# An audio layer whose first norm's factor is carried by the second norm's epsilon: what it does to the time

## The reference, cut to what matters

```
x = x * rsqrt(mean(x^2) + 1e-6) * w_pre        # per token, over 2560
h = x @ w1.T                                   # 1024 numbers
g = silu(h[512:]) * h[:512]                    # gate times value
y = g @ w2.T                                   # 1024 numbers
y = y * rsqrt(mean(y^2) + 1e-6) * w_post       # per token
```

## Time and profile before

| | us |
|---|---|
| median of 3 runs | 2608.62 |
| the 3 runs | 2606.7 to 2609.98 |
| the profiled execution's own time | 2612.99 |
| its span, first to last instruction | 2611.3 |
| PE busy in the span | 2454.8 (94%) |
| DVE busy in the span | 1663.6 (64%) |
| mean granted clock of PE | 0.97 of full speed |

### The profile page before, as it was taken

One profiled execution on the slowest core, in us unless ns is written; L12 is line 12 of the kernel. 1 busy time (PEld: TensorE's weight loads), 2 busy tenths in 40 slices (PEclk: granted clock), 3 DMA queues, 4 the chain that ended last, 5 costly groups with the idle time before them and its releaser, 6 DMA issues. The chain is left out here.

```text
span 2611.3 us, 45875 instructions
## 1 busy us (share of the span) xinstructions
PE 2454.8 (94%) x15004; PEld 2124.4 (81%) x15004; DVE 1663.6 (64%) x3316; ACT 1191.6 (46%) x3624; POOL 984.6 (38%) x852
## 2 busy tenths in 40 slices
PE   8999999986899978999999999799999998899998
PEld 6888788875566658899999999678888886899998
DVE  8875587893466658889999898621111112877775
ACT  5664445441344448898989898611111111111110
POOL 5764677771122226666666666200000000111110
PEclk9999999997899989999999999899999999899999
DMA  7654677676456541111111110453333332211211
GB/s 253 199 166 146 190 247 250 210 230 235 129 177 210 187 140 65 45 44 44 41 46 42 45 46 36 143 166 97 96 96 96 96 96 81 89 65 65 81 65 49
DMA packets 202314, 313.61 MB, mean 120 GB/s; under 512 B 20784, under 2 KB 157488, under 8 KB 202032
## 3 DMA queue, kind: packets, MB, share of 16 engines
q1 hardware_dynamic: 194256, 282.54, 33.8%
q0 software_dynamic: 7184, 25.69, 2.5%
q10 hardware_dynamic: 720, 3.67, 0.4%
HBM read 230.05 MB, written 81.79 MB: 119 GB/s over the span
## 5 line engine op out<-in xcount | busy, mean ns | idle before, releaser
L1508 ACT ACTIVATE attn_prob<-attn_prob,attn_bias 94x94 f32<-94x94 f32 x1024 | 367.3, 361 | 57.3 <-DVE attn_bias L1585 57.2
L1867 POOL TENSOR_TENSOR ffn_res<-shared_h,ffn_bias 128x1024 f32<-128x1024 f32 x24 | 59.8, 2494 | 852.9 <-DMA ffn_bias<-base_b 558.0
L740 PE MATMUL up_ps<-up_t_lo,up_s_hi 128*128 128x502 f32 (+1 forms) x840 | 332.8, 396 | 23.4 <-DVE up_t_lo L655 23.4
L741 PE MATMUL up_ps<-up_t_hi,up_s_lo 128*128 128x502 f32 (+1 forms) x840 | 329.3, 392 | 0.0
L742 PE MATMUL up_ps<-up_t_hi,up_s_hi 128*128 128x502 f32 (+1 forms) x840 | 328.8, 391 | 0.0
L1717 DVE TENSOR_TENSOR out_x_lo<-out_raw,out_x_hi 128x512 fp32r<-128x512 f32 x96 | 66.5, 692 | 400.8 <-ACT out_x_hi L1702 400.8
L506 POOL TENSOR_TENSOR up_both<-up_raw 128x502 f32<-128x502 f32 (+1 forms) x150 | 240.1, 1604 | 116.0 <-DVE up_t_lo L655 86.3
L1624 POOL TENSOR_TENSOR attn_prob<-attn_prob,attn_share 94x752 f32<-94x752 f32 x128 | 184.5, 1442 | 218.9 <-DVE attn_share L1593 218.9
L1702 ACT ACTIVATE out_x_hi<-out_raw 128x512 fp32r<-128x512 f32 x96 | 60.6, 632 | 434.7 <-PE out_ps_h L243 283.8
L243 PE MATMUL out_ps_h<-out_w_hi,out_x_lo 128*128 128x512 f32 x768 | 238.6, 392 | 12.4 <-DVE out_w_lo L228 12.4
L243 PE MATMUL out_ps_h<-out_w_lo,out_x_hi 128*128 128x512 f32 x768 | 238.1, 391 | 0.0
(11 more groups left out here) (227 smaller groups left out, 5801.1 us busy)
## 6 DMA issues: line engine op xcount, KB each, us to landing
up_raw<-x_f SPq DMA_DIRECT2D x240, 251.0 KB, 3.3
up_w_raw<-w SPq DMA_DIRECT2D x120, 256.0 KB, 3.9
up_raw<-x_f SPq DMA_DIRECT2D x120, 250.0 KB, 3.5
out_raw<-o_t SPq DMA_DIRECT2D x96, 256.0 KB, 4.4
o_t<-attn_o_t SPq DMA_DIRECT2D x128, 188.0 KB, 1.9
shared_ring<-wo SPq DMA_DIRECT2D x32, 512.0 KB, 6.6
y<-down_y POOLq DMA_DIRECT2D x24, 512.0 KB, 3.4
out_y<-y SPq DMA_DIRECT2D x24, 512.0 KB, 5.7
```

Of the source, the lines that this page charges most:

```text
L740: nc.tensor.matmul(o, sh, tl, start=(kk == 0), stop=False)
L741: nc.tensor.matmul(o, sl, th, start=False, stop=False)
L1508: last = nc.scalar.activation(prob[u % NPR][0:SEQ, h, part], prob[u % NPR][0:SEQ, h, part], ACT.Exp, bias=bias[u % 2][0:SEQ, n:n + 1], sca ...
```

## The change

It does four things.

1. The second multiplication by rate (`GATE_LAST`, L689, six of them) is gone; `VALUE` waits for the silu instead.
2. DVE writes 1e-6 * v of all tokens into a small tile `eps` (126 x 24) in group 13, and SP stores it to a table of 3072 numbers in HBM: one store for each column, at steps 150 to 173, each of 126 numbers (124 or 122 for the last of a chunk), one number from each partition. At the stage's end SP writes ones for the 64 tokens of padding.
3. At the start of `down`, SP loads the table into `own`, 128 partitions by 24 numbers. In HBM the numbers of one partition lie 128 apart, so that each of the 3072 is a piece of 4 bytes. The load stands behind the four pieces of w2 and ahead of the four small tables.
4. ACT's root and DVE's sum take their epsilon from `own`, in the column of the tile's number, which in the loop is a register.

```
-        GATE_FIRST, GATE_LAST, VALUE = {}, {}, {}
+        GATE_FIRST, VALUE = {}, {}
...
+            def store_eps(n):
+                c, j = n // 4, n % 4
+                a, w = TOKC[c]
+                lead = 0 if j < 3 else 4 * SUB - w
+                at = a + SUB * j
+                sp.dma_start(d["eps"][at:at + SUB - lead, :], eps[lead:SUB, n:n + 1]).then_inc(eps_stored, 16)
...
                 if s in begins:
                     load_weights(begins[s])
+                n = s - KH * (STAT_AT + 2)
+                if n == 0:
+                    sp.wait_ge(eps_done, 1)
+                if 0 <= n < 24:
+                    store_eps(n)
...
             sp.wait_ge(zero_set, 1)
+            sp.wait_ge(ones_set, 1)
+            sp.dma_start(d["eps"][TOK:TOKP, :], ones[0:TOKP - TOK, 0:1]).then_inc(eps_stored, 16)
...
+            sp.wait_ge(eps_stored, 16 * 25)
...
                     dve.sem_inc(stat_taken, 1)
+                    nc.vector.tensor_scalar(eps[0:SUB, :], var[0:SUB, 0, :], RMS_EPS, None, ALU.mult).then_inc(eps_done, 1)
...
-                if s in GATE_LAST:
-                    c = GATE_LAST[s]
-                    dve.wait_ge(silu_done, nth_gate[c] + 1)
-                    nc.vector.tensor_tensor(half(c, HIGH), half(c, HIGH), rate(c), ALU.mult).then_inc(rate_done, 1)
                 if s in VALUE:
                     c = VALUE[s]
-                    dve.wait_ge(rate_done, nth_last[c] + 1)
+                    dve.wait_ge(silu_done, nth_gate[c] + 1)
...
+        own = mem.sb("own", [P, TILES])
...
                         for n in range(NW):
                             ws.load(sp, n)
+                        with nc.allow_non_contiguous_dma("one number a token"):
+                            sp.dma_start(own[:], d["eps"].rearrange("(t p) one -> p (t one)", p=P)).then_inc(own_in, 16)
                         for dst, name in ((post, "post_ln"), (kvw, "kv_ln"), (qln, "q_ln"), (post_col, "post_col")):
...
-                    nc.scalar.activation(root[b][:, 0:1], ms[b][:, 0:1], ACT.Sqrt, bias=eps[:, 0:1]).then_inc(yroot_done, 1)
+                    if first(t, 1):
+                        act.wait_ge(own_in, 16)
+                    nc.scalar.activation(root[b][:, 0:1], ms[b][:, 0:1], ACT.Sqrt,
+                                         bias=own[:, bass.ds(t, 1)]).then_inc(yroot_done, 1)
...
-                    nc.vector.tensor_scalar(v[:, 0:1], ms[b][:, 0:1], RMS_EPS, -0.5, ALU.add, ALU.mult)
+                    nc.vector.tensor_scalar(v[:, 0:1], ms[b][:, 0:1], own[:, bass.ds(t, 1)], -0.5, ALU.add, ALU.mult)
```

More of the change, by code:

```diff
@@ L329, in tok_up @@
         r = mem.sb("r", [P, 24])
+        eps = mem.sb("eps", [P, 24])
         var = mem.sb("var", [P, 3, 24])
@@ L356, in tok_up @@
         silu_done = mem.sem("silu_done")
-        rate_done = mem.sem("rate_done")
+        eps_done = mem.sem("eps_done")
+        eps_stored = mem.sem("eps_stored")
         g_done = mem.sem("g_done")
@@ L410, in tok_up @@
         RATE_AT = {group(4, 2): (0, 1), group(5, 0): (2, 3), group(5, 1): (4, 5)}
-        GATE_FIRST, GATE_LAST, VALUE = {}, {}, {}
+        GATE_FIRST, VALUE = {}, {}
         for pr in range(PAIR):
             GATE_FIRST[KH * group(5, pr + 1) + 0] = 2 * pr
-            GATE_LAST[KH * group(5, pr + 1) + 4] = 2 * pr
             GATE_FIRST[KH * group(5, pr + 2) + 1] = 2 * pr + 1
-            GATE_LAST[KH * group(5, pr + 2) + 5] = 2 * pr + 1
             VALUE[KH * group(5, pr + 2) + 8] = 2 * pr + 1
@@ L421, in tok_up @@
         nth_gate = {GATE_FIRST[s]: n for n, s in enumerate(gates)}
-        lasts = sorted(GATE_LAST)
-        nth_last = {GATE_LAST[s]: n for n, s in enumerate(lasts)}
         values = sorted(VALUE)
@@ L803, in tok_down @@
         eps = mem.sb("eps", [P, 1])
+        own = mem.sb("own", [P, TILES])
+        own_in = mem.sem("own_in")
         eps_set = mem.sem("eps_set")
@@ L2188 @@
          for n, a in arrays.items()}
-    for n, shape in (("wq_pair", (PAIRS, P, 2, 2 * P)), ("wvo", (P, PAIRS, DM)), ("g_t", (P, 4, TOKP)),
+    for n, shape in (("wq_pair", (PAIRS, P, 2, 2 * P)), ("wvo", (P, PAIRS, DM)), ("g_t", (P, 4, TOKP)), ("eps", (TOKP, 1)),
                      ("y", (TILES, P, DM)), ("o_t", (P, PAIRS, TOKP)), ("h", (TILES, P, DM))):
```

## The result

| | before | after |
|---|---|---|
| median of 4 runs of each (us) | 2608.91 | 2658.17 |
| the 4 runs | 2606.7 to 2609.98 | 2650.66 to 2660.58 |
| span of the profiled execution | 2611.3 | 2656.0 |
| mean granted clock of PE | 0.970 | 0.964 |

The ratio is 1.0186, with an interval of 1.0168 to 1.0204: the changed kernel is 49 us slower, far outside the predicted range. Where the 44.7 us between the two profiled executions lie is read from SP's issues. The first tile of g in `down` is issued at 667.69 instead of 626.35, the second tile 21.70 us after the first instead of 19.76, and the first load of attention's tables 330.76 us after that instead of 329.11 (1020.15 and 975.22 us). From there to the end it is 1635.9 us against 1636.1. So 41.3 us are lost in `up`, 1.9 at the start of `down`, 1.7 in the rest of it, and none behind it.

What follows compares the result with a forecast made beforehand. PE was taken to bound `up`, and transfers with one chain behind them the start of `down`. The terms -9.0 + 0.5 + 5.4 + 1.0 gave -2.1 us, so 2606.5 us, with 2600 to 2614.5 for 8 in 10.

Steps and rivals of the forecast that it cites:

- What bounds the kernel: In `up`, PE is the bound, busy 594 of 630 us; DVE time counts only where PE waits for it.
- Part 1, -9.0: In `up`, six multiplications less on DVE shorten PE's waits: a gain of 9.0 us, low end 5.0.
- 608 to 609.5: Sign of being right: the time in us at which the last matmul of `up` would start.
- a stall of 0.3 to 2.1 us: PE's wait for DVE in `up` said to remain after the multiplications are removed.
- the 11.2 us: PE's whole loss late in `up`, from step 170 on: all that a faster DVE could give back.
- Part 2, +0.5: Making and storing the table in `up` costs 0.5 us, ends 0 and 4.
- the high bound: For the stores in `up`: 73 ns a packet, the queue's mean; at ten in a row 0.7 us a store.
- The cover: In `up`, POOL's and PE's leads were said to hide 0.7 us a store.
- Rival 3: Stores hold up x loads around steps 169 to 173, losing the regained lead: +3, 2611.5 us; chance 0.08.
- Part 3, +5.4: At the start of `down`, the table's load delays the second tile of g and PE by 5.4 us, ends 0.8 and 12.8.
- the cheap rival: The table's load in `down` is nearly free, 0.8 us: -6.7 in all, 2601 us; chance 0.29.
- Part 4, +1.0: In the loop of `down`, register operands on ACT and DVE cost 1.0 us, ends 0 and 2.2.

Runs made afterwards that it cites:

- mul_only: The kernel before with only the six second multiplications removed and VALUE waiting for the silu; 2601.62 us, ratio 0.9986.
- stores_spaced: The changed kernel without the table's load, its stored 4-byte numbers 64 bytes apart in HBM instead of side by side; 2607.91 us, ratio 0.9997.
- rows_far: The changed kernel without the table's load, each store writing 16 rows of 8 numbers, rows 512 bytes apart in HBM; 2606.18 us, ratio 0.9997.
- rows_near: As rows_far, but with the 16 rows of 8 numbers side by side, 512 bytes to a store; 2654.75 us, ratio 1.019.
- stores_32: The changed kernel without the table's load, its stored 4-byte numbers 32 bytes apart in HBM; 2604.65 us, ratio 0.9983.
- load_only: The changed kernel with its load of 3072 pieces, but the table written by one store of 128 rows of 96 bytes; 2610.73 us, ratio 1.0008.
- rate_row: The changed kernel, whole function, with r stored once as a row from one partition and DVE making 1e-6/r^2 after the load; 2610.69 us, ratio 1.0009.
- col_copied: row_loaded, but with the table loaded as 3072 pieces of 4 bytes as in the changed kernel; 2606.54 us, ratio 1.0006.
- row_loaded: rate_row with the table loaded as 24 rows of 512 bytes, turned by PE, and POOL copying each tile's column to a fixed place; 2602.18 us, ratio 0.9978.
- reg_only: The kernel before with only the epsilon operand changed, to a column picked by the tile's number, all 1e-6; 2612.63 us, ratio 1.0025.

## Why the prediction was wrong

**What bounds the kernel: right.** PE is the bound in `up` as long as x comes in time, and DVE's multiplications were worth time where PE waited.

**Part 1, -9.0: right mechanism, smaller.** Measured alone it is -6.1 us in the profile, and -3.7 by the ratio. The last matmul of `up` starts at 611.36 in mul_only, where 608 to 609.5 was given as the sign. The forecast left a stall of 0.3 to 2.1 us and, at worst, 1.7 for the clock. In mul_only both came: 2.3 us of waits, and a granted clock of 0.91 from 540 to 560 us, (1 - 0.91) x 20 = 1.8 us. Of the 11.2 us that leaves 7.1, and 1.0 more stays without a row. (From 535 to 540 the clock was at 1.00, as forecast.) POOL was not freed as hoped, since the other multiplication by rate, L685, stays and POOL's sum beside it is as long as ever. From mul_only, in order of time:

```profile
524.91 3.35 DVE L685 TENSOR_TENSOR up_c_t<-up_c_t,up_ssq 128x2008 f32<-128x2008 f32 x1
526.10 3.28 POOL L506 TENSOR_TENSOR up_both<-up_raw 128x502 f32<-128x502 f32 x1
```

**Part 2, +0.5: the step that failed.** The text priced a store at "nothing" to "73 ns" a packet, "at ten in a row 0.7 us a store, which POOL's and PE's leads cover". It is the price that was wrong. With stores the step takes 4.64 us, where it took 2.72; x lands late, and POOL's waits for it rise from 8.7 to 73.0 us, where the text had expected "no new wait of POOL for x".

In the terms of the text: a step of 4.64 us at a share of 0.97 is 4.5 us on each transfer engine; before, it was 2.72 x 0.68 = 1.85. So one store adds 2.65 us on each of 16 engines, 42 us in all for 126 numbers, or 0.34 us a number, over four times the high bound. Almost none of this stands in the packets of the numbers, whose mean is 11.4 ns; it is the packets of x that grew from 102 to 256 ns in the mean. The bound came from the mean packet of the queue, and the low end from short packets that pass quickly. They did pass quickly. A packet's own time, short or mean, says nothing of what it does to the packets beside it, and stores_spaced and rows_far show that the price hangs on where the writes fall.

The cover was reckoned for one late load, and 24 stores at one a step are a rate. But at the text's own price the rate would have fitted too: 1.85 + 0.7 = 2.55 us of a step of 2.72. At 2.65 it doesn't, and no lead helps. That the excess, 1.8 us, times 24 is 43 us, near the 41.3 + 6.1 = 47.4 us that `up` lost against mul_only, is no second proof, since the 2.65 was itself taken from the longer steps.

Rival 3 had the mechanism, stores that hold up x, but placed it at two stores of 122 numbers and gave it +3. It is all 24, and +47. It had leaned on the Trainium skill ("DMA: Bandwidth & Descriptors", "Specifications"), by which transfers under 512 bytes are done by read-modify-write. Being under 512 bytes is not by itself what costs time here: pieces of 4 bytes 64 bytes apart and pieces of 64 bytes side by side are both under it and lose nothing. The Trainium skill's "Collectives: The Full Stack" ("Rules for kernel authors") asks that buffers of collectives be aligned to 32 bytes, against read-modify-write. That doesn't decide here either: the rows of rows_near begin 32 bytes apart, as the numbers of stores_32 do, and the first lose 48 us and the second nothing.

**Part 3, +5.4: smaller, and by another way.** From the first issue of g to PE's restart, the four kernels with the load of 3072 pieces take 43.06 (the changed kernel), 43.81, 43.85 and 43.84 us (load_only, rate_row, col_copied), the fourteen without it 40.25 to 42.95, mean 41.5 (before 41.79). The load costs about 2 us there, near the cheap rival. In whole times it is less clear: col_copied is 4.4 us above row_loaded in the medians. The text took 6.6 us for the load's packets and let the transfers behind it wait for that backlog, and wrote that "SP itself isn't late". The packets took about 2 us, which the text had named as a sign of being wrong, and the second tile of g lands no longer after its issue than before (ACT starts on it 6.03 us after, against 6.77). It was SP that became late: it is held for 12.17 us at the issue behind the load. The 7.5 us that it used to wait ahead of `wo` are gone, and it issues the second tile 1.9 us later, counted from the first.

**Part 4, +1.0: too small.** It is +6.5 us in the medians and +3.3 in the `down` of reg_only's profile; the high end was 2.2. The other 3.2 us are not located. The fourteen profiled kernels with the register operand take 306.5 to 316.4 us from PE's restart to attention's tables, mean 310.5; the four without it 306.4 to 309.6, mean 307.7. The ranges overlap, so it is the number of waits that separates the two groups. The term counted the waits of PE that existed and not those that would arise: twelve at L1198's place, which had one before. ACT's folded copy stands behind the root in ACT's order, and was just in time. The register operations sum to 18 x (43 + 46) ns = 1.6 us and DVE's slower operation to 24 x 60 ns = 1.4; DVE's part is unlikely to be the cause, since row_loaded and col_copied have the same 214 ns (with a fixed column) and are among the four of 307.7. ACT's root takes 294 ns in both. That leaves the register operations, by exclusion and not by a run of their own.

**The sum.** With these values and stores that cost nothing it is -6.1 + 2 + 3.3 = -0.8 us, where -2.1 was forecast; rate_row, which is that kernel, measured 1.0009 (0.9996 to 1.0021), which is -1.0 to +5.5 us. So without its 24 stores the change lies in the stated range, though not at the forecast of -2.1. That it comes so near is partly luck: the gain and the load were put too high, the register too low. The miss is the stores alone.

## What to carry to other kernels

Before you call a row of transfers hidden, treat it as a rate: add its time on each transfer engine to what the stage already needs, and compare the sum with the length of a step, not with a lead. The sum is only as good as the price, and the time of a short packet isn't its price: look at what the packets beside it take. Don't store a column of SBUF as single numbers side by side in HBM; find a row that holds the same values in one partition, leave 16 bytes or more between the numbers, or store and load whole rows and turn them on PE. Where an operation is lengthened in the order of an engine, ask which waits are now at zero behind it, not only which are above it.

## What was not expected of the hardware

- 24 stores of 126 numbers of 4 bytes within 504 bytes of HBM each cost 60 us of a stream of loads (1.0232), with transfer engines busy at 0.96. The writes' own packets take 9 to 12 ns in the mean, against 9.0 to 9.1 in the cheap kernels; it is packets of the loads that take up to 7.7 us. Spread over 2 KB or more, the same number of writes cost nothing (1.0, 0.9983, 0.9997).
- A shared 32-byte stretch isn't the decisive thing: 16 rows of 8 numbers cost 48 us within 512 bytes and nothing over 8 KB. The size of the stretch that must not be crowded is open from 64 to 512 bytes, and whether it is a bank, a channel or another part of the memory that is crowded, no run here tells. Between 512 bytes and 2 KB to a store nothing was tried.
- 113 numbers a store cost 155 us, more than twice the 60 of 122 to 126, with the loads behind each store taking 8 us to issue. By the packet counts they go to one transfer engine instead of 14.
- A load of 3072 pieces of 4 bytes is through in about 2 us, but holds the next issue of its queue for 12.17 us, behind w2.
